# Sharing one bank and handing GpSimd half of the finishing work in a four-layer graph network

## The reference

```python
h0 = (adj @ x + x) / (sum(adj, 1) + 1)                       # layer 0
y0 = relu(concat([x, h0]) @ W + b);  y0 = y0 / norm(y0)
y1 = tanh(concat([x, t]) @ W1 + b1) @ W2 + b2 \
     + adj @ (x @ B.T) - sum(adj, 1) * (x @ B.T)             # layer 1
rank = cumsum(adj != 0, 1); k = min(rank[:, -1:], 100)       # layer 2
w = (adj != 0) * where(rank > deg - k, 0.5 ** (k - pos), 0)
y2 = w @ (x @ weight) + bias
y3 = logmap(adj @ expmap(x)) @ kernel + bias                 # layer 3
x = layernorm(x + y)                                         # after each
```

## Time and profile before

| | us |
|---|---|
| median of 3 runs | 173.23 (172.87 to 173.72) |
| the profiled execution | 172.62 |
| its span | 170.8 |

### The profile page before, as it was taken

One profiled execution on the slowest core, in us unless ns is written; L12 is line 12 of the kernel. 1 busy time (PEld: TensorE's weight loads), 2 busy tenths in 40 slices (PEclk: granted clock), 3 DMA queues, 4 the chain that ended last, 5 costly groups with the idle time before them and its releaser, 6 DMA issues.

```text
span 170.8 us, 3082 instructions
## 1 busy us (share of the span) xinstructions
PE 110.9 (65%) x1230; PEld 63.5 (37%) x1244; DVE 105.7 (62%) x235; ACT 70.8 (41%) x119; POOL 46.3 (27%) x54
## 2 busy tenths in 40 slices
PE   0000279961996498669725979999989989994000
PEld 0000159730243124326402345667446734463000
DVE  0181999889999998950499101535602698718870
ACT  0030215577277556462781285254023310157550
POOL 0000002412421263020148000433500554603380
PEclk9999999997599789999985899999999999999755
DMA  4999999999999910000000000000000000000005
GB/s 97 255 250 345 307 347 263 319 331 333 332 331 339 341 40 4 0 0 4 0 4 0 0 0 4 0 4 2 0 4 0 0 2 0 0 4 0 0 0 123
DMA packets 13950, 18.73 MB, mean 110 GB/s; under 512 B 5360, under 2 KB 5488, under 8 KB 13936
## 3 DMA queue, kind: packets, MB, share of 16 engines
q1 hardware_dynamic: 7728, 9.74, 20.1%
q10 hardware_dynamic: 6208, 8.78, 17.5%
HBM read 18.00 MB, written 0.52 MB: 108 GB/s over the span
## 4 chain that ended last, share of the span: by engine, by line
PE 44%; DVE 26%; ACT 9%; DMA 7%; issue 4%; POOL 4%; SPq 2%; POOLq 1%; another core or an unknown queue 0%; DVEq 0%
PE psN L823 7%; PE psC L823 7%; DMA stage<-adj 7%; PE psS L823 6%; PE psS L880 5%; DVE AT L572 5%; DVE AT L573 4%; ACT WT L402 3%; PE psX L940 2%; POOL nroot L308 2%; PE psX L872 2%; PE psX L852 2%; PE psC L861 2%; PE psH L970 2%; PE psH L971 2%
## 5 line engine op out<-in xcount | busy, mean ns | idle before, releaser
L402 ACT ACTIVATE WT<-psC 128x1024 int16<-128x1024 f32 x32 | 31.3, 1021 | 17.2 <-PE psC L919 17.2
L289 POOL TENSOR_TENSOR root<-var,power 128x4 f32<-128x4 f32 (+1 forms) x16 | 18.9, 1183 | 46.8 <-DVE var L622 22.6
L823 PE MATMUL psS<-AT,XP 128*128 128x512 bf16 x74 | 20.4, 398 | 1.2 <-issue 1.1
L572 DVE STREAM_TRANSPOSE AT<-stage 128x1024 bf16<-128x1024 bf16 x10 | 13.1, 1311 | 11.7 <-DMA stage<-adj 11.7
L872 PE MATMUL psH<-AT,cb 128*32 128x256 bf16 x32 | 1.7, 344 | 19.3 <-DVE AT L573 19.3
L573 DVE STREAM_TRANSPOSE AT<-stage 128x1024 bf16<-128x1024 bf16 x10 | 12.7, 1275 | 0.0
L823 PE MATMUL psN<-AT,XP 128*128 128x512 bf16 x44 | 12.0, 402 | 1.0 <-DVE XP L578 0.7
L638 DVE TENSOR_TENSOR t<-psH,XB 128x256 f32<-128x256 f32 x4 | 1.7, 424 | 17.5 <-PE psH L971 10.2
L823 PEld LDWEIGHTS psS<-AT,XP 128*128 128x128 f16 x80 | 7.3, 101 | 12.4 <-issue 5.9
L302 POOL TENSOR_TENSOR XB<-X,weights 128x256 f32<-128x256 f32 x12 | 9.9, 835 | 7.0 <-DVE X L627 7.0
L914 PE MATMUL psC<-later,cb 32*32 32x512 bf16 x256 | 7.2, 398 | 6.0 <-ACT WT L402 6.0
(11 more groups left out here) (151 smaller groups left out, 229.5 us busy)
## 6 DMA issues: line engine op xcount, KB each, us to landing
stage<-adj SPq DMA_DIRECT2D x20, 256.0 KB, 15.2
stage<-adj ACTq DMA_DIRECT2D x20, 256.0 KB, 11.5
WT<-adj ACTq DMA_DIRECT2D x12, 256.0 KB, 12.7
WT<-adj SPq DMA_DIRECT2D x12, 256.0 KB, 16.9
out<-X SPq DMA_DIRECT2D x6, 64.0 KB, 1.9
weights<-weights_packed SPq DMA_DIRECT2D x1, 353.5 KB, 15.7
cb<-constants_packed SPq DMA_DIRECT2D x1, 264.2 KB, 9.8
X<-x SPq DMA_DIRECT2D x2, 128.0 KB, 7.1
```

The lines of the kernel that those rows point to most:

```text
L289: nc.gpsimd.tensor_tensor(root[:, e, 0:n], var[:, e, 0:n], power[:, 0:n, 0:NR], ALU.pow).then_inc(root_ready, 1)
L402: nc.scalar.activation(WT[:, e, tiles], psC[:, PAIRS * h:PAIRS * (h + 1)], ACT.Relu).then_inc(chain_taken, 1)
L572: nc.vector.transpose(to[:, :, :, :, 0], halves[:, :, 0, :, :, 1])
L823: ins = nc.tensor.matmul(sum_bank(l, e), XP[:, l % 2, c], matrix, start=(c == 0), stop=last)
```

## The change

1. **One bank.** Counts, spread table and degrees of all chunks use `psH`, where the dense products of layer 0 are too. `dense(0, e)` now waits until the degrees have been read, and `counts(e)` until the dense product before has been read. `psX` is left to the transpositions of x and the hidden products.
2. **GpSimd does part of chunks 0 and 1.** The square, the centring, the three combining operations with their square, and the making of X run on GpSimd (`square_relu`, `centre_relu`, `combine`, `scale_rows`). VectorE keeps relu, the sums over features and the split (`relu0`, `sums0`, `variance0`, `split1`). Chunks 2 and 3 keep `activate0`, `combine0`, `normalise`.
3. **Start.** The lower half of piece 1 is issued ahead of the constants, piece 3 ahead of the large weights. Centring x moves from VectorE to GpSimd. Of the seven weight blocks only b1 is centred early, the six others before the last `normalise(0, 3)`.
4. **Order.** TensorE, ScalarE and VectorE get new lists: the last counts come before the second hidden product, and the chain steps are spread otherwise.

```diff
-CENTRED = ("W2", "BT", "WL2", "b1", "b2", "b3", "K")
+CENTRED = ("b1", "W2", "BT", "WL2", "b2", "b3", "K")
...
+            load_lower(1)
             sp.dma_start(cb[:].bitcast(U16), cpack).then_inc(consts_loaded, 16)
             sp.dma_start(weights[:, 0:first], wpack[:, 0:first]).then_inc(own_weights_loaded, 16)
-            for m in range(1, NR - 1):
+            for m in range(2, NR):
                 load_lower(m)
...
+            def square_relu(e):
+                pool.wait_ge(y_ready, e + 1)
+                ye = v[:, chunk(e), 0:D]
+                nc.gpsimd.tensor_tensor(X[:, chunk(e)], ye, ye, ALU.mult).then_inc(ysq_ready, 1)
+
+            def centre_relu(e):
+                pool.wait_ge(ymean_ready, e + 1)
+                ye = v[:, chunk(e), 0:D]
+                step(nc.gpsimd.tensor_tensor(ye, ye, per_node(ymean[:, chunk(e)]), ALU.add))
+
+            def combine(e):
+                te = t[:, chunk(e)]
+                pool.wait_ge(ssroot_ready, e + 1)
+                step(nc.gpsimd.tensor_tensor(te, v[:, chunk(e), 0:D], per_node(ssroot[:, chunk(e)]), ALU.mult))
+                step(nc.gpsimd.tensor_tensor(te, te, XB[:, chunk(e)], ALU.add))
+                nc.gpsimd.tensor_tensor(X[:, chunk(e)], te, te, ALU.mult).then_inc(tsq_ready, 1)
+
+            def scale_rows(e):
+                pool.wait_ge(root_ready, e + 1)
+                nc.gpsimd.tensor_tensor(X[:, chunk(e)], t[:, chunk(e)], per_node(root[:, e, 0]), ALU.mult
+                                        ).then_inc(x_ready, 1)
...
+            pool.wait_ge(xmean_ready, 1)
+            nc.gpsimd.tensor_tensor(XB[:], X[:], per_node(xmean[:]), ALU.add).then_inc(xc_ready, 1)
             pool.wait_ge(own_weights_loaded, 16)
-            for e in range(NE):
+            add_bias(0)
+            weigh(0)
+            for e in range(1, NE):
                 add_bias(e)
+            pool.wait_ge(xc_ready, 1)
             pool.wait_ge(consts_loaded, 16)
             for e in range(NE - 2):
-                weigh(e)
+                square_relu(e)
+                centre_relu(e)
                 l2_root(e)
+                combine(e)
                 var_root(0, e)
+                scale_rows(e)
+                weigh(e + 1)
                 diagonals(e)
                 residual(1, e)
...
+            def sums0(e):
+                cs = chunk(e)
+                dve.wait_ge(y_ready, e + 1)
+                step(nc.vector.tensor_reduce(ymean[:, cs], v[:, cs, 0:D], AX_X, ALU.add))
+                nc.vector.tensor_scalar(ymean[:, cs], ymean[:, cs], -1.0 / D, None, ALU.mult).then_inc(ymean_ready, 1)
+                dve.wait_ge(ysq_ready, e + 1)
+                step(nc.vector.tensor_reduce(ss[:, cs], X[:, cs], AX_X, ALU.add))
...
             add_own_part(2)
             transposes(15)
             activate0(2)
             take_degrees(3)
+            combine0(2)
             add_own_part(3)
             activate0(3)
-            combine0(2)
+            normalise(0, 2)
             combine0(3)
-            normalise(0, 2)
+            centre("W2", "K")
             normalise(0, 3)
...
             def counts(e, cols=slice(0, CW)):
-                if e == NE - 1:
-                    pe.wait_ge(hid_taken, 2)
-                bank = psH if e == 0 else psX
+                if e >= 1:
+                    pe.wait_ge(dense_taken, e)
...
                 if l == 0:
+                    pe.wait_ge(deg_taken, e + 1)
```

More of the change, by code:

```diff
@@ L269, in _, with step @@
         def _(pool):
+            steps = [0]
+            def step(ins):
+                steps[0] += 1
+                ins.then_inc(pool_step, 1)
+                pool.wait_ge(pool_step, steps[0])
+            def square_relu(e):
[16 more added lines that the diff above has]
+                                        ).then_inc(x_ready, 1)
             def add_bias(e):
@@ L592, in add_own_part, with relu0, variance0, split1 @@
                 nc.vector.tensor_tensor(t[:, chunk(e)], rows, Z[:, chunk(e)], ALU.add).then_inc(dense_taken, 1)
+            def relu0(e):
+                dve.wait_ge(dense_taken, e + 1)
+                nc.vector.tensor_scalar(v[:, chunk(e), 0:D], t[:, chunk(e)], 0.0, None, ALU.max).then_inc(y_ready, 1)
+            def sums0(e):
[5 more added lines that the diff above has]
+                step(nc.vector.tensor_reduce(ss[:, cs], X[:, cs], AX_X, ALU.add))
+                nc.vector.tensor_tensor(ss[:, cs], ss[:, cs], floor[:, cs], ALU.max).then_inc(ss_ready, 1)
+            def variance0(e):
+                dve.wait_ge(tsq_ready, e + 1)
+                step(nc.vector.tensor_reduce(var[:, e, 1], X[:, chunk(e)], AX_X, ALU.add))
+                nc.vector.tensor_scalar(var[:, e, 0], var[:, e, 1], 1.0 / D, LN_EPS, ALU.mult, ALU.add
+                                        ).then_inc(var_ready, 1)
+            def split1(e):
+                dve.wait_ge(x_ready, e + 1)
+                split(1, e, X[:, chunk(e)], PART_SCALE[1])
+            def centre(first, last):
+                k = CENTRED.index(last) - CENTRED.index(first) + 1
+                rows = W(first, last).rearrange("p (k f) -> p k f", f=D)
+                step(nc.vector.tensor_reduce(wmean[:, 0:k], rows, AX_X, ALU.add))
+                nc.vector.scalar_tensor_tensor(rows, wmean[:, 0:k].unsqueeze(2).to_broadcast([P, k, D]), -1.0 / D,
+                                               rows, ALU.mult, ALU.add).then_inc(centred, 1)
             def activate0(e):
@@ L713, in _ @@
                                            ALU.mult, ALU.subtract).then_inc(parts_ready, 1)
-            for m in range(2, 4):
+            for m in range(2, 5):
                 transposes(m)
@@ L718, in _ @@
                                            ).then_inc(h_bias_ready, 1)
[L719 to L723 removed]
+            centre("b1", "b1")
             transposes(5)
@@ L993, in _ @@
             sum_cols(0, 0, 2)
+            pe.wait_ge(transposed, 4)
+            counts(0, second)
             transpose_x(0, 1)
+            sum_cols(0, 2, 4, spread_first)
             own_part(0)
+            degrees(0)
             transpose_x(0, 2)
             own_part(1)
+            dense(0, 0)
             transpose_x(0, 3)
@@ L1000, in _ @@
             own_part(3)
-            pe.wait_ge(transposed, 4)
-            counts(0, second)
-            sum_cols(0, 2, 4, spread_first)
-            degrees(0)
             chain(0)
-            dense(0, 0)
             chain(1)
-            chain(2)
             for e in range(1, NE - 1):
                 pe.wait_ge(transposed, NR * (e + 1))
-                pe.wait_ge(deg_taken, e)
                 counts(e)
@@ L1042, in _ @@
             sum_cols(e, 3, 4)
+            transpose_x(1, 1)
+            spread(e)
+            sums(1, 0, range(1, 2))
+            degrees(e)
             chain(10)
-            spread(e)
-            degrees(e)
             dense(0, e)
-            sums(1, 1, range(0, 1))
+            hidden(1)
             chain(11)
-            sums(1, 1, range(1, 2))
+            sums(1, 1, range(0, 2))
             chain(12)
@@ L1052, in _ @@
             sums(1, 0, range(2, 3))
+            chain(13)
             hidden(2)
             sums(1, 1, range(2, 3))
-            chain(13)
+            chain(14)
             sums(1, 0, late)
@@ L1062, in _ @@
             dense(1, 0)
-            chain(14)
+            chain(15)
             sums(1, 2, every)
@@ L1066, in _ @@
             dense(1, 1)
-            chain(15)
             sums(1, 3, every)
```

121 lines of the change are left out of this document (55 added, 66 removed).

## The result

The changed kernel takes 165.62 us (median of four runs, 164.29 to 165.97), the kernel before, on the same chip, 173.06 (172.87 to 173.72). The ratio is 0.955, 95% interval 0.949 to 0.961: 4.5% faster. Forecast were 164.6 and 161.6 to 168.6. The profiled execution of after took 164.29 us, its span is 162.5 us; of before 172.62 and 170.8. In every ratio, executions more than 1.5% above the fastest of their kernel are left out; medians are of all executions.

The account below looks back on a forecast made before the run. Up to 73 us VectorE bounds the kernel, then the path to layer 2's dense product at 102.0. Gains 8.1 + 0.5 = 8.6 us off the profiled 172.62 give 164.0, median 164.6; range 161.6 to 168.6.

Parts of the forecast that it names:

- 1, start: Start of kernel: piece 1 lands earlier, its transpose near 14 us, piece 4's at 28.1; centring x on GpSimd 3.3 us; cost 0.
- 2, T6: VectorE's transpose of piece 6 (128 rows of adj) starts at 33.9 us, 0.9 earlier than before.
- 3, offload: Chunks 0 and 1: moving six operations to GpSimd saves VectorE 2.4 us each; variance sums ready with 1.3 us to spare.
- rival C: Offload does not unload: VectorE waits for GpSimd as long as it saved; gain about 4, 169.3 us; chance 0.11.
- 4, new waits: Chunk 1: shared bank and lower TensorE clock delay its degrees to 48.5 us; VectorE waits 2.6; piece 10's transpose at 49.7.
- 5, split: Split of X beside GpSimd's diagonals and residual: 0.7 us more per chunk, 1.9 if both halves are held.
- 6, last chunk: TensorE's new order starts the last counts at 69.6 us, before the last transpose ends; degrees at 76.3, 6.1 earlier.
- 7, degrees to layer 2: Last degrees to layer 2's first dense product: 1.4 us wait for chunk 2's root, dense at 93.9, 8.1 earlier.
- D: Slower: lower TensorE clock from last degrees to layer 2's first dense product, 11.7 us later, 176.3 us; chance 0.06.
- 8: After layer 2's first dense product: one chain step less on TensorE, 0.5 us.
- A: Small gain: the new waits also hit chunk 2 and the last counts, last transpose hardly moves; 168.6 us; chance 0.13.
- B: Large gain: TensorE gets full clock early and GpSimd never holds VectorE; 161.7 us; chance 0.10.

Follow-up runs that it names:

- the second execution of the kernel: The changed kernel run again with nothing changed, as yardstick of the experiments: 165.44 us, ratio 0.953 to the kernel before.
- the first experiment: Changed kernel, but VectorE again does square, centring, combining and making of X of chunks 0 and 1: 168.41 us, ratio 0.971 to the kernel before.
- the kernel with the root order: Changed kernel with GpSimd taking chunk 2's variance root ahead of chunk 3's norm root, last diagonals ahead of chunk 3's variance root: 164.53 us, ratio 0.949 to before.
- start and own parts: Changed kernel with SP's old transfer order, and own parts 2, 3 and the first chain step ahead of chunk 0's dense product: ratio 0.946 to before.

## Why the prediction held, step by step

**1, start.** T1 (13.48, forecast 14) and T4 (27.64; 28.1) as forecast, XB on GpSimd 1.89 us and not 3.3. The step that failed is "cost 0". It asked whether VectorE or GpSimd is held back and did not ask what a TensorE does that is fed earlier: it waits longer, 3.38 us, and the clock falls. The new start costs 1.7 to 3.3 us, some 2 of it by the clock, and that sits in part 4. T4 itself came early by luck: 27.64 is the earliest of eight.

**2, T6.** 33.50 for 33.9.

**3, offload.** T7 37.05 (37.2), T8 41.69 (41.1), T9 ended 46.6 (45.9). GpSimd's operations of 128x256 took 0.61 to 0.73 us, not 0.83, but the square of chunk 0 waited behind the last two bias additions until 40.51 and VectorE waited 0.58 us for it (1.57 in the second execution of the kernel). The forecast's spare cover of 1.3 us concerned the variance, which VectorE never waited for; it did not ask about the square. Worth 3.0 us in all, as the first experiment shows; rival C had little for it.

**4, new waits.** Dense product at 33.69 (33.9), step 0 39.80 (38.0), counts of chunk 1 43.93 (41.2), degrees 50.43 (48.5), VectorE's wait 4.11 (2.6), T10 51.71 (49.7). Queue and order of the steps were right; mis-sized was the lower clock, taken only from the counts of chunk 1 on. It held already for the dense product and the own parts, 0.7 + 1.6 us, and for the steps. Without it the forecast's times come out: counts at 40.93 where the start is undone.

**5, split.** The second half took 1.15 us in both chunks, 0.43 when GpSimd's diagonals are out of its way: 0.7 for each chunk, as forecast. The Trainium skill (SBUF — State Buffer, Who interferes with whom) states that a VectorE instruction with two SBUF inputs contends with a GpSimd instruction that reads SBUF, and calls the lock exclusive. The trace agrees for the second half: it began at 54.39, 0.26 us after GpSimd's diagonals, and ended 0.27 us after them. The first half has one input and was not held (0.25 us) where it began together with the diagonals, 54.11 and 54.13. So it is 0.7 and not 1.9; but where they had begun 0.23 us earlier, at the end of the layer in the kernel with the root order, the first half took 1.01 us, so which half is held goes by who starts first. From T10 to T15 went 17.9 us, forecast were 19.1.

**6, last chunk.** Last counts 69.98 (69.6), sums ended 75.0 (74.6), degrees 76.48 (76.3). The hidden product put back ahead of the counts cost 3.9 us: the gain is order, as argued. What was lost at T10 had been won back by the degrees of chunk 2: its counts began at 58.76, 1.8 us later than forecast (57.0), and its degrees came at 63.61, only 0.2 later (63.4). The forecast took 6.4 us for this, with the lower clock as in before (counts 1.90); at full clock (counts 1.05) it took 4.85. Behind it TensorE goes by its own order and not by T15.

**7, degrees to layer 2.** Wait for the root 1.38 (1.4), parts of chunk 3 90.6 (90.2), dense product 94.1 (93.9). In before it started at 101.74, so the gain is 7.6 us for a forecast 8.1: the forecast set 93.9 against the end of the last hidden product, which comes at 94.3 here and at 101.9 in before. ScalarE's row ended at 91.6, forecast 91.0, and "both lead to about the same point" is right within about 0.5 us, by the root experiment. Full clock throughout, so D had nothing for it here; its mechanism showed only in single hidden products of this stretch, 1.99 us with the diagonals later and 2.07 with start and own parts, at a cost of some 0.8 us.

**8.** From the first residual 0.7 us less, forecast 0.5.

The sum by the trace: 7.6 at the dense product and 0.7 behind it give a span 8.3 us shorter; forecast 8.6. The median fell by 7.4, 1.2 less than the forecast. The later landing of piece 4 in other executions is a likely cause, since it came 1.5 us later in the second profiled one and the span was 1.2 longer; for the executions without a trace it is not shown. That the total came out is partly luck, because two errors about the clock cancelled. It was low earlier and longer than forecast at chunk 1, so that T10 was 2.0 us late; and it was full at chunk 2, where the forecast had it low, so that the last counts were late by only 0.4 and the last degrees by 0.2. VectorE caught up 1.2 us from T10 to T15, mostly because it did not meet the forecast wait for the degrees of chunk 2. Of the rivals, A had the place right (T15 moves by only 0.9 us against before) and the consequence wrong; B's full clock came at chunk 2, and ahead of chunk 1's counts only with the transfers put back, own parts first or the idle time filled; D's stretch kept the full clock.

## What to carry to other kernels

An engine that is fed earlier is not for free: if it only waits longer for somebody else, its clock may fall just when the work on the critical path arrives, so cost every earlier transfer by where the engine's idle time then lies. When an edit both delays a result and reorders the queue that waits for it, the two are one edit; taken alone the offload lost 9 us. And look for a milestone behind which the schedule is rigid (here T10, 44.4 us to layer 2 in five executions of three kernels): it tells at once which half of the program an experiment has touched.
